# First load of a GNN layer's item projection regrouped, with two warming passes fewer

## What is computed

```python
def reference(x, adj, item_feat, W_item, b_item, W_user, b_user):
    h = item_feat @ W_item.T + b_item          # 10000 x 128
    b = x @ W_user.T + b_user                  # 10000 x 128
    y = x + relu(adj @ h + b)                  # adj: 10000 x 10000
    m = mean(y, axis=-1, keepdims=True)
    v = var(y, axis=-1, keepdims=True)
    return (y - m) / sqrt(v + 1e-05)
```

## Time and profile before

| | |
|---|---|
| median of 3 runs | 1084.77 us (1084.77 to 1084.8) |
| the profiled execution's own time | 1085.42 us |
| its span | 1083.6 us |
| PE busy (matmul) | 1078.2 us, 99% |
| DVE, ACT, POOL busy | 961.6, 837.2, 116.2 us |
| mean rate of the transfers | 385 GB/s |
| granted TensorE clock, mean | 0.999 |

### The profile page before, as it was taken

The page is one execution under the profiler, slowest core; times in us unless marked ns, Lnnn a source line. Parts: engine busy times, 40 slices in busy tenths (PEclk is TensorE's granted clock), DMA queues, the critical chain, the costliest instruction groups (busy, mean ns, idle before and its releaser), DMA issues.

```text
span 1083.6 us, 14879 instructions
## 1 busy us (share of the span) xinstructions
PE 1078.2 (99%) x4937; PEld 901.4 (83%) x4937; DVE 961.6 (89%) x613; ACT 837.2 (77%) x802; POOL 116.2 (11%) x56
## 2 busy tenths in 40 slices
PE   9999999999999999999999999999999999999998
PEld 9888888888888888888888888888888888888888
DVE  6999898989898989898989898989898989898987
ACT  6878877878777777787878787878787878787775
POOL 4360000000000000000000000000000000000001
PEclk9999999999999999999999999999999999999999
DMA  9999999999999999999999999999999999999993
GB/s 377 420 378 422 372 422 357 422 369 422 372 422 344 422 364 423 354 423 361 422 358 422 359 423 360 422 357 422 361 422 361 423 353 423 366 422 351 421 350 155
DMA packets 66264, 417.14 MB, mean 385 GB/s; under 512 B 8178, under 2 KB 9012, under 8 KB 19908
## 3 DMA queue, kind: packets, MB, share of 16 engines
q1 hardware_dynamic: 65668, 415.76, 96.2%
q10 hardware_dynamic: 576, 1.11, 0.3%
HBM read 411.72 MB, written 5.12 MB: 385 GB/s over the span
## 4 chain that ended last, share of the span: by engine, by line
PE 99%; DVE 0%; DVEq 0%; issue 0%
PE acc L458 32%; PE acc L464 32%; PE acc L457 32%; PE h_ps L440 2%; PE acc L461 0%; PE z_ps L431 0%; DVE stats L784 0%; DVE items L807 0%; DVE items L800 0%; PE z_ps L472 0%; DVE moments L791 0%; DVEq L201 0%; DVE items L741 0%; PE h_ps L444 0%; DVE rstd L796 0%
## 5 line engine op out<-in xcount | busy, mean ns | idle before, releaser
L717 DVE TENSOR_TENSOR adj_lo<-adj,adj_hi 128x2048 fp32r<-128x2048 f32 (+2 forms) x391 | 864.7, 2230 | 106.5 <-ACT adj_hi L519 105.8
L519 ACT CAST adj_hi<-adj 128x2048 fp32r<-128x2048 f32 (+2 forms) x391 | 725.3, 1865 | 146.8 <-DMA adj<-adj_t 83.0
L457 PE MATMUL acc<-adj_hi,h_hi 128*128 128x512 f32 (+1 forms) x1580 | 604.3, 384 | 0.0
L458 PE MATMUL acc<-adj_hi,h_lo 128*128 128x512 f32 (+1 forms) x1580 | 604.3, 384 | 0.0
L464 PE MATMUL acc<-adj_lo,h_hi 128*128 128x512 f32 (+1 forms) x1580 | 417.2, 384 | 0.0
L457 PEld LDWEIGHTS acc<-adj_hi,h_hi 128*128 128x128 f32 x1580 | 296.6, 188 | 58.6
L458 PEld LDWEIGHTS acc<-adj_hi,h_lo 128*128 128x128 f32 x1580 | 296.5, 188 | 58.4
L464 PEld LDWEIGHTS acc<-adj_lo,h_hi 128*128 128x128 f32 x1580 | 292.5, 188 | 58.5
L670 POOL TENSOR_TENSOR items<-items,minus_mean 128x512 f32<-128x512 f32 x19 | 39.2, 2065 | 586.3 <-ACT minus_mean L562 586.3
L674 POOL TENSOR_TENSOR items<-items,rstd_all 128x512 f32<-128x512 f32 x19 | 37.6, 1979 | 341.0 <-ACT rstd_all L583 341.0
L554 ACT COPY gathered<-part 32x16 f32<-32x16 f32 x152 | 30.8, 203 | 19.0 <-DVE part L755 11.5
(11 more groups left out here) (51 smaller groups left out, 154.4 us busy)
## 6 DMA issues: line engine op xcount, KB each, us to landing
adj<-adj_t SPq DMA_DIRECT2D x360, 1024.0 KB, 7.7
adj<-adj_t SPq DMA_DIRECT2D x21, 512.0 KB, 5.2
adj<-adj_narrow SPq DMA_DIRECT2D x11, 952.0 KB, 7.7
xg<-x_t SPq DMA_DIRECT2D x19, 256.0 KB, 8.0
out<-items SPq DMA_DIRECT2D x19, 256.0 KB, 2.2
tail_in<-adj_tail SPq DMA_DIRECT2D x57, 32.0 KB, 4.4
adj<-item_t SPq DMA_DIRECT2D x2, 512.0 KB, 6.9
adj<-item_t SPq DMA_DIRECT2D x1, 1024.0 KB, 9.4
```

The costliest lines, as they stand in the source:

```text
L457: nc.tensor.matmul(into, h_hi[:, k, :], high[:, c, :], start=(k == 0), stop=False)
L458: nc.tensor.matmul(into, h_lo[:, k, :], high[:, c, :], start=False, stop=False)
L519: nc.scalar.copy(into[:, places[0]:places[-1] + 1, :], source[:, places[0]:places[-1] + 1, :]).then_inc(hi_made, 1)
L717: nc.vector.tensor_tensor(into[:, places[0]:places[-1] + 1, :], source[:, places[0]:places[-1] + 1, :], high[:, places[0]:places[-1] + 1, ...
```

## The change

The projection's weights now lie in one tile with the items, `w_and_items`, ahead of the first block. One load, `w_first_items`, still the first on SP, brings the weights and the first two chunks of block 0: 384 values (1.5 KB) on each of 128 partitions, 192 KB. Item load 0, still ACT's first, brings the other two chunks of block 0, 128 KB in place of 256. The bias rows are a load of their own, `bias_rows`, 64 KB, issued by ACT behind item loads 0 and 2 and ahead of load 4. PE waits for the first load before block 0's first product and for item load 0 before its third. DVE waits for the bias where it waited for the weights and bias. `WARM` is 7 in place of 8, so 14 passes in place of 16. The core of the diff, without the renaming of `w_item[:, :]` and `bias_item`:

```diff
-WARM = 8
+WARM = 7
...
-ACT_LOADS = (0, 2, 4)
-ITEM_RANGES = [(a * PER_TILE * P, min(b * PER_TILE * P, N_ITEM)) for a, b in ITEM_LOADS]
+FIRST_ITEMS = PER_TILE // 2 * P
+ACT_LOADS = (0, 2)
+ACT_LOADS_BEHIND_BIAS = (4,)
+ITEM_RANGES = [(max(a * PER_TILE * P, FIRST_ITEMS), min(b * PER_TILE * P, N_ITEM)) for a, b in ITEM_LOADS]
...
-        items = sb("items", [P, OWN_SLOTS, PER_TILE * P])
-        w_bias = sb("w_bias", [P, 2 * HID])
+        w_and_items = sb("w_and_items", [P, HID + OWN_SLOTS * PER_TILE * P])
+        bias_item = sb("bias_item", [P, HID])
...
+        w_item = w_and_items[:, 0:HID]
+        items = w_and_items[:, HID:].rearrange("p (s n) -> p s n", s=OWN_SLOTS)
...
-            return item_t[P * first:P * end].rearrange("(p n) -> p n", p=P)
+            return item_t[P * (first - FIRST_ITEMS):P * (end - FIRST_ITEMS)].rearrange("(p n) -> p n", p=P)
...
             first, end = ITEM_RANGES[n]
-            return item_tiles(ITEM_LOADS[n][0], end - first), item_rows(first, end)
+            a = ITEM_LOADS[n][0]
+            skip = first - a * PER_TILE * P
+            return item_tiles(a, skip + end - first)[:, skip:], item_rows(first, end)
...
-            sp.dma_start(w_bias[:, :], w_item_bias).then_inc(w_bias_landed, 16)
+            sp.dma_start(w_and_items[:, 0:HID + FIRST_ITEMS], w_first_items).then_inc(w_first_landed, 16)
...
-                if n not in ACT_LOADS:
+                if n not in ACT_LOADS + ACT_LOADS_BEHIND_BIAS:
                     load_items(n)
...
-                pe.wait_ge(item_landed[item_load(t)], 16)
+                if t > 0:
+                    pe.wait_ge(item_landed[item_load(t)], 16)
                 if t >= H_PS_RING:
                     pe.wait_ge(h_full_made, t - H_PS_RING + 1)
                 n = full_chunks(t)
                 for c in range(n):
+                    if t == 0 and c * P == FIRST_ITEMS:
+                        pe.wait_ge(item_landed[0], 16)
...
             warm_up()
-            pe.wait_ge(w_bias_landed, 16)
+            pe.wait_ge(w_first_landed, 16)
...
             for n in ACT_LOADS:
+                act.dma_start(*item_load_places(n)).then_inc(item_landed[n], 16)
+            act.dma_start(bias_item[:, :], bias_rows).then_inc(bias_landed, 16)
+            for n in ACT_LOADS_BEHIND_BIAS:
                 act.dma_start(*item_load_places(n)).then_inc(item_landed[n], 16)
...
-            dve.wait_ge(w_bias_landed, 16)
+            dve.wait_ge(bias_landed, 16)
```

More of the change, by code:

```diff
@@ L197, in parts, with gnn_kernel @@
     return [(tile_places(g, t), steps)]
-def gnn_kernel(nc, adj_t, adj_tail, x_t, adj_narrow, tail_narrow, x_narrow, item_t, w_item_bias, w_user_t, b_user, out, out_last):
+def gnn_kernel(nc, adj_t, adj_tail, x_t, adj_narrow, tail_narrow, x_narrow, item_t, w_first_items, bias_rows, w_user_t, b_user, out, out_last):
     with ExitStack() as ctx:
@@ L246, in gnn_kernel @@
         squares = items[:, 3, :].rearrange("p (n j) -> p n j", j=SQ)
-        w_item = w_bias[:, 0:HID]
-        bias_item = w_bias[:, HID:2 * HID]
         acc = [psum(f"acc{i}", [P, 512]) for i in range(2)]
@@ L261, in gnn_kernel @@
         x_landed = sem("x_landed")
-        w_bias_landed = sem("w_bias_landed")
+        w_first_landed = sem("w_first_landed")
+        bias_landed = sem("bias_landed")
         w_user_landed = sem("w_user_landed")
@@ L310, in item_tiles @@
             if at < OWN_SLOTS:
-                return items[:, :, :].rearrange("p s n -> p (s n)")[:, at * PER_TILE * P:at * PER_TILE * P + cols]
+                at = HID + at * PER_TILE * P
+                return w_and_items[:, at:at + cols]
             slot, at = divmod(at - OWN_SLOTS, PER_TILE)
@@ L439, in project_items @@
                 for c in range(n):
+                    if t == 0 and c * P == FIRST_ITEMS:
+                        pe.wait_ge(item_landed[0], 16)
                     mm = nc.tensor.matmul(h_ps[t % H_PS_RING][:, c, :], item_tiles(t, PER_TILE * P)[:, c * P:c * P + P],
-                                          w_item[:, :], start=True, stop=True)
+                                          w_item, start=True, stop=True)
                 if t == LAST:
                     pe.wait_ge(items_tail_made, 1)
-                    mm = nc.tensor.matmul(h_ps[t % H_PS_RING][:, n, :], items_tail[:, :], w_item[:, :],
+                    mm = nc.tensor.matmul(h_ps[t % H_PS_RING][:, n, :], items_tail[:, :], w_item,
                                           start=True, stop=True)
@@ L690, in add_item_bias @@
                 if t == LAST:
-                    nc.vector.tensor_tensor(h_tail[:, :], h_ps[t % H_PS_RING][:, n, :], bias_item, ALU.add)
+                    nc.vector.tensor_tensor(h_tail[:, :], h_ps[t % H_PS_RING][:, n, :], bias_item[:, :], ALU.add)
                 nc.vector.tensor_tensor(h_full[:, k:k + n, :], h_ps[t % H_PS_RING][:, 0:n, :],
@@ L879 @@
         "item_t": np.concatenate([items[:, a:b].ravel() for a, b in ITEM_RANGES]),
-        "w_item_bias": np.concatenate([np.asarray(L0_gnn_W_item).T,
-                                       np.broadcast_to(np.asarray(L0_gnn_b_item), (P, HID))], axis=1),
+        "w_first_items": np.concatenate([np.asarray(L0_gnn_W_item).T, items[:, :FIRST_ITEMS]], axis=1),
+        "bias_rows": np.broadcast_to(np.asarray(L0_gnn_b_item), (P, HID)).copy(),
         "w_user_t": np.ascontiguousarray(np.asarray(L0_gnn_W_user).T),
```

## The result

The changed kernel takes 1086.39 us (median of 22 runs, 1085.8 to 1088.83). The kernel before takes 1085.01 us in the 22 runs beside it (1084.62 to 1085.92). The ratio is 1.0014, with a 95% interval of 1.0008 to 1.0020: slower by 1.4 us, and within the 0.2% named as the bound for no change. The profiled execution took 1086.61 us, its span is 1084.8 us against 1083.6.

A forecast was written before the change was run, and what follows sets the result against it. TensorE (PE), busy 1078.2 of 1083.6 us, was taken as the bound. From 1084.77 us a gain of 0.10 at the head was taken off, other terms charged nothing: 1084.67 us, range 1084.45 to 1086.4.

The forecast's parts named there:

- PE's unbroken chain: Whole span: nothing stops PE between its first pass and the end, so head gains or losses pass on whole.
- The first load: SP's load of weights and half of block 0: landing L = 3.94 us, at most 4.14; gain 0.10 us.
- The head start: Second projection pass 0.20 us earlier, up to 0.52; worth 0.10 us after the clock's rise, at most 0.27.
- rival c: Hole before the first projection delays TensorE's rise from 6.8 to 10.2 us: 1.6 us less the gain, 1086.3; chance 0.20.
- The bias: ACT's third load: lands by about 7.9 us at latest, and even then no delay reaches PE.
- The cover: Ring of four product buffers between PE and DVE; without it up to 1.65 us of waiting for the bias.
- what was to be seen: DVE's first addition starts at about 6.2 us, released by PE and not by the bias load.
- The later item loads: Loads behind the first ones: load (4, 6) at worst lands at 8.8 us, needed by 8.82; nothing charged.
- The stream as a whole: All transfers: 128 more rows cost 0.15 us, at most 0.72, covered at the second tile of adj.
- Rival b: A load becomes PE's wait at block 4 or 1, 0.1 to 0.3 us late: 1084.8 to 1085.0; chance 0.05.
- The rule on interleaving queues: First pair of loads: bytes moved from ACT's to SP's buy nothing; L = 3.98, a gain of 0.08 us.
- a same within 0.2%: Whole kernel: time within 0.2%, 2.2 us, of the kernel before; chance 0.96.

The follow-up runs named there:

- bias with half: Changed kernel with the bias rows behind block 0's second half in ACT's first load (192 KB): 1086.19 us, ratio 1.0010; the repeat, one execution, 1086.13 us.
- old loads, 14 passes: The kernel before with two warming passes fewer (14), loads untouched: 1084.81 us, ratio 0.9997.
- the bias load behind (4, 6): Changed kernel with the bias load behind block 4's load on ACT's queue: 1087.83 us, ratio 1.0026; the repeat, one execution, 1089.21 us.

## Why the prediction was wrong, point by point

- **PE's unbroken chain** The earlier trace rows was right: 1.2 us of hole and gain at the head came out as 1.2 us of span.
- **The first load** was too late in the forecast: L = 3.94 expected, 3.6 measured, inside the range (3.6 was the point below which nothing is waited for). The taken row, the old first load, had a partner of 256 KB in 2 KB rows beside it. Read to the end, my own argument of 128 KB less on the other queue would have given an earlier landing. The head start was therefore the full one, 0.28 us for 0.27. The sentence that bytes moved between the two first loads buy nothing doesn't hold either: with the same 384 KB as two loads of 192 KB (bias with half) both are there at 3.8, where it was 4.15.
- **The rise of the clock** (rival c) did not move: 6.8 us in the profiled execution, in which there was no hole to test the rival. It also came at 6.7 us with the 0.53 us from pass to pass before the first product (old loads, 14 passes), and none of that kernel's 11 runs was 1.6 us longer. That a hole of that size delays the rise isn't borne out. The range's upper end was put by this rival, and the measured 1086.39 us lies just inside, by luck: another cause put it there.
- **The bias** landed at 7.4, inside its bound of 7.9, and cost PE nothing: the first of DVE's additions, the one that block 4 needs, was over by 8.1, before its due time of 8.87. But DVE was released by the bias load and not by PE, against what was to be seen. The cover was right at 7.4 and is gone at 9.1, as the bias load behind (4, 6) shows.
- **The step that failed** is "The later item loads". The bound said that load (4, 6) is at worst as late as load (6, 8) was, 8.6, and 0.16 us for 64 KB: 8.8. It landed at 10.2. The bound took a landing of the old trace as fixed, while that load itself moved to 9.9 under the change. It also left out that load (6, 8) starts earlier when the rows beside load (3, 4) are small ones. "The stream as a whole" gave 0.15 us for 128 more rows, at most 0.72; the pair of loads was 1.5 us later. Costs per packet from averages over the whole span don't hold in the first microseconds.
- **Rival b**, a load that becomes the wait at block 4, is what happened. It had a chance of 0.05 and a price of 0.1 to 0.3 us; the price was 1.4 to 1.5. Its bound left 0.02 us of margin (8.80 against 8.82), and a margin of that size deserved a chance near one half.
- **The rule on interleaving queues** of the Trainium skill (page "DMA: Bandwidth & Descriptors", section "Issuing engines are not separate DMA queues"), cited for the first pair, bore on the later loads too and was not applied there. It says that the queues' transfers interleave; that two loads of 512 KB then finish together, and the earlier issue doesn't keep one ahead, is what the runs add (10.2 and 9.9 us here, 7.9 and 8.7 before).
- The forecast of a same within 0.2% held.

## What to carry to other kernels

When loads are put in a just-in-time order on two queues, a change of the first loads moves every later pair. Write down for each load what stands beside it on the other queue, and when it is due, and don't bound a landing by one read in the old trace. A head start of PE is worth nothing beyond the first load that isn't early too; here it could have been 0.28 us at best, and what it put at risk was 1.5. An extra small load in front of a due one can cost far more than its bytes: look at the rows that it puts beside the other queue's, and at what that queue then starts sooner.

## What had not been expected of the hardware

- 64 KB more on ACT's queue moved a load of 512 KB behind it by 1.8 us (7.9 to 9.7), where its bytes are 0.16 us at 400 GB/s.
- The clock's rise is not at a fixed place: with PE at work from 0.78 us in every execution, the spacing of the passes changed at 6.7 to 6.9 us in seven of the 18 traces and at places from 3.8 to 6.1 us in the other eleven. An early rise brings PE to block 4 before its load and so gives nothing to the changed kernel.
- Single holes of 1.9 us at most (from pass to pass) were not followed by a fall of the clock; after holes of 2.2, 2.3, 2.3 and 3.2 us, and after two holes of 1.8 and 0.9 us close together, it fell to 0.50 for 3.4 us. A wait of PE for a load can so cost 1.6 us on top of itself.
